# W_v and W_o folded into one product per head, summed into x by VectorE, with the later steps four half slots earlier

## What is computed

```python
# cross attention, on the normalised x, per batch
q = (query @ w_q).reshape(B, Q, 16, 64).transpose(0, 2, 1, 3)   # likewise k, v
scores = jnp.einsum('bhqd,bhkd->bhqk', q, k) * scale
attn = jax.nn.softmax(scores, axis=-1)
out = jnp.einsum('bhqk,bhkd->bhqd', attn, v)
return out.transpose(0, 2, 1, 3).reshape(B, Q, 16 * 64) @ w_o

# the routed tree, for four trees q, k, v and f
for _ in range(8):
    logit = jnp.einsum('bsd,bsd->bs', x, nw[node]) + nb[node]
    node = 2 * node + 1 + (logit > 0).astype(jnp.int32)
leaf = node - 255
h = act(jnp.einsum('bsd,bsdl->bsl', x, w1[leaf]) + b1[leaf])
return jnp.einsum('bsl,bsld->bsd', h, w2[leaf]) + b2[leaf]
```

## Time and profile before

| | us |
|---|---|
| median of 3 runs | 752.05 |
| lowest and highest run | 750.29, 752.97 |
| span of the profiled execution | 754.4 |
| PE busy in it | 597.3 (79%) |
| DVE busy | 546.0 (72%) |
| ACT busy | 406.1 (54%) |
| POOL busy | 240.9 (32%) |

### The profile page before, as it was taken

One profiled execution on the slowest core, in us unless ns is written; L12 is line 12 of the kernel. 1 busy time (PEld: TensorE's weight loads), 2 busy tenths in 40 slices (PEclk: granted clock), 3 DMA queues, 4 the chain that ended last, 5 costly groups with the idle time before them and its releaser, 6 DMA issues.

```text
span 754.4 us, 10417 instructions
## 1 busy us (share of the span) xinstructions
PE 597.3 (79%) x3928; PEld 521.6 (69%) x3928; DVE 546.0 (72%) x876; ACT 406.1 (54%) x903; POOL 240.9 (32%) x184
## 2 busy tenths in 40 slices
PE   3799999999999979779999997799999858530020
PEld 3588898899988868668978886689888747310010
DVE  2466665676666798986787798967777997737955
ACT  2476566667565557466556666665648534311420
POOL 3110000211021246740141459510523346276503
PEclk9899999999999998899999998999999989755555
DMA  9410000110000053300300174000300243034403
GB/s 230 162 40 1 2 1 1 39 45 31 1 1 1 1 199 98 107 1 1 116 2 0 40 265 158 1 1 1 116 1 2 66 168 116 1 116 168 181 0 119
DMA packets 21105, 49.03 MB, mean 65 GB/s; under 512 B 1472, under 2 KB 14144, under 8 KB 16960
## 3 DMA queue, kind: packets, MB, share of 16 engines
q0 software_dynamic: 4608, 34.74, 12.7%
q1 hardware_dynamic: 15760, 13.31, 6.2%
q10 hardware_dynamic: 688, 0.33, 0.2%
HBM read 48.10 MB, written 0.26 MB: 64 GB/s over the span
## 4 chain that ended last, share of the span: by engine, by line
PE 56%; DVE 28%; ACT 6%; issue 5%; POOL 3%; DMA 2%; ACTq 0%; DVEq 0%; POOLq 0%
PE ps_s L316 20%; PE ps_av L316 16%; PE ps_ring L427 12%; DVE chunk_max L855 5%; DVE tree L735 5%; DVE hid L714 4%; PE ps_m L316 4%; DVE pt_lo L679 3%; PE ps_ring L316 3%; DVE cur L699 3%; ACT prob L609 2%; ACT pt_hi L649 2%; DVE tree L679 1%; DVE hid L679 1%; DMA ident<-ident_in_dram 1%
## 5 line engine op out<-in xcount | busy, mean ns | idle before, releaser
L679 DVE TENSOR_TENSOR pt_lo<-ps_ring,pt_hi 128x512 fp32r<-128x512 f32 x256 | 169.7, 685 | 102.0 <-ACT pt_hi L649 102.0
L649 ACT CAST pt_hi<-ps_ring 128x512 fp32r<-128x512 f32 x256 | 145.1, 591 | 142.0 <-PE ps_ring L427 141.9
L427 PE MATMUL ps_ring<-ident,prob 128*128 128x128 f32 x1024 | 150.6, 280 | 34.4 <-DVE pt_lo L679 12.8
L609 ACT ACTIVATE prob<-ps_s,neg_max 128x1024 f32<-128x1024 f32 x128 | 141.6, 1113 | 52.2 <-DVE neg_max L876 52.0
L427 PEld LDWEIGHTS ps_ring<-ident,prob 128*128 128x128 f32 x1024 | 121.6, 146 | 65.6 <-issue 49.3
L855 DVE TENSOR_REDUCE chunk_max<-ps_s 128x1 f32<-128x1024 f32 x128 | 150.5, 1214 | 7.1 <-PE ps_s L316 7.0
L316 PE MATMUL ps_av<-pt_hi,c_hi 128*128 128x256 f32 x512 | 151.8, 296 | 0.0
L316 PE MATMUL ps_av<-pt_lo,c_hi 128*128 128x256 f32 x512 | 145.2, 284 | 0.0
L316 PE MATMUL ps_av<-pt_hi,c_lo 128*128 128x256 f32 x512 | 145.1, 283 | 0.0
L316 PE MATMUL ps_s<-ct_hi,q_hi 128*128 128x512 f32 x256 | 116.3, 454 | 4.9 <-ACT prob L609 3.9
L316 PE MATMUL ps_s<-ct_lo,q_hi 128*128 128x512 f32 x256 | 104.9, 410 | 0.0
(11 more groups left out here) (216 smaller groups left out, 739.8 us busy)
## 6 DMA issues: line engine op xcount, KB each, us to landing
stage<-ctx_t_dram SPq DMA_DIRECT2D x16, 256.0 KB, 3.1
stage<-ctx_rows_dram SPq DMA_DIRECT2D x16, 256.0 KB, 3.0
wv<-w_v_dram SPq DMA_DIRECT2D x1, 512.0 KB, 11.7
wo<-w_o_dram SPq DMA_DIRECT2D x1, 512.0 KB, 12.0
dec<-decay_dram SPq DMA_DIRECT2D x1, 512.0 KB, 7.8
nw<-node_w_dram SPq DMA_DIRECT2D x1, 510.0 KB, 8.5
nb<-node_b_dram SPq DMA_DIRECT2D x1, 510.0 KB, 8.9
wsm<-w_small_dram SPq DMA_DIRECT2D x1, 448.0 KB, 11.6
```

Of the source, the lines that this page charges most:

```text
L427: last = nc.tensor.transpose(o[:, i * P:(i + 1) * P], prob[:, n % 2, k:k + P], ident[:])
L609: nc.scalar.activation(prob[:, n % 2, 1024 * e:1024 * (e + 1)], ps_s[:, 1024 * e:1024 * (e + 1)], ACT.Exp, bias=neg_max[:, n:n + 1], accum ...
L649: nc.scalar.copy(pt_hi[:, pp, row:row + KPC, P * (n % 2):P * (n % 2 + 1)], ps_ring[:, i % 2, :].rearrange("p (k q) -> p k q", k=KPC))\
L679: return nc.vector.tensor_tensor(o, a, b_, op)
```

## The change

It computes the same in another way:
- A product `wvo` of W_v and W_o is made for each head in slots 2 to 16: PE transposes four heads of W_v (`turn0` to `turn3`, slots 2, 6, 10, 14) and multiplies by W_o (`join0` to `join3`, slots 4, 8, 12, 16), both in `ps_m` and copied by ACT at the slot's end. `wv` and `wo` are loaded into the leaf buffers, `wo` with 64 partitions.
- The odd X holds `av_sb` times `wvo`, 128 columns a head, and DVE adds it straight into `x_sb` with two SCALAR_TENSOR_TENSOR (L885, L887: PSUM times `rsum` plus x), at the top of the even slot, and frees the buffer.
- `o_sb`, `ot_sb`, the transposition, the step `proj` and the addition in `x1` are gone.
- All half-slot numbers of the later steps are 4 smaller, two slots. The numbers of `split_ct` and `split_c` are not in the tables and stay.

```diff
-POOL_AT = dict(of="Pool", xn1=45, rope=48, mask_q=48, gate=52, xl=55, xf=56, cur=57, gather_up01=59,
-               gather_down01=59, up0=61, up1=63, gather_up2=64, down0=65, gather_down2=66, up2=66, down1=67, down2=69, cur_f=72, gather3=77,
+POOL_AT = dict(of="Pool", xn1=41, rope=44, mask_q=44, gate=48, xl=51, xf=52, cur=53, gather_up01=55,
+               gather_down01=55, up0=57, up1=59, gather_up2=60, down0=61, gather_down2=62, up2=62, down1=63, down2=65, cur_f=68, gather3=73,
...
+VALUE_PE = {2: "turn0", 4: "join0", 6: "turn1", 8: "join1", 10: "turn2", 12: "join2", 14: "turn3", 16: "join3"}
...
+            def value_products(k):
...
+                    for h in range(4):
+                        last = nc.tensor.transpose(ps_m[0:DH, h * D:(h + 1) * D],
+                                                   wv[:, DH * (4 * i + h):DH * (4 * i + h + 1)], ident[:])
+                    last.then_inc(S["wv_turned"], 1)
+                else:
+                    pe.wait_ge(S["wvt_ready"], i + 1)
+                    for h in range(4):
+                        last = mm(ps_m[:, h * D:(h + 1) * D], wv_t[:, h, :], wo[:, 4 * i + h, :])
...
-                    if ot_pair(s) is not None:
-                        pe.wait_ge(S["ring_taken"], BY_ACT[("X", s - 1, 0)])
-                        last = nc.tensor.transpose(o[:, 256:256 + P], o_sb[:].rearrange("p a b -> p (a b)"), ident[:])
...
-                            last = mm(o[:, DH * j:DH * (j + 1)], av_sb[:, j * P:(j + 1) * P],
-                                      wv[:, DH * h:DH * (h + 1)])
+                            last = mm(o[:, j * P:(j + 1) * P], av_sb[:, j * P:(j + 1) * P], wvo[:, h, :])
...
+                if o_pair(s - 1) is not None:
+                    pair, i = o_pair(s - 1), RING[("X", s - 1, 0)]
+                    mine = x_sb[:, pair // PPB, :]
+                    dve.wait_ge(S["ring_filled"], i + 1)
+                    dve.wait_ge(S["rsum_ready"], pair + 1)
+                    if wqk_pair(s - 1) is not None:
+                        dve.wait_ge(S["ring_taken"], BY_ACT[("X", s - 1, 0)])
...
+                    link(nc.vector.scalar_tensor_tensor(mine, ps_ring[:, i % 2, 0:P], rsum[:, 2 * pair:2 * pair + 1],
+                                                        mine, ALU.mult, ALU.add))
+                    nc.vector.scalar_tensor_tensor(mine, ps_ring[:, i % 2, P:2 * P], rsum[:, 2 * pair + 1:2 * pair + 2],
+                                                   mine, ALU.mult, ALU.add).then_inc(S["ring_free"], 1)
```

## The result

The changed kernel takes 782.9 us (median of 4 runs, 780.1 to 784.7), the kernel before 752.5 us beside it (4 runs). The ratio is 1.040, 95% interval 1.035 to 1.044. It is slower, as forecast, but by 30 us where I had 18, and 1.9 us above the end of the range.

What follows compares the result with a forecast made beforehand. PE was taken to bound clean slots and DVE those with tree work. The terms summed to +17.8 us on the 754.4 us span, 772.2, less 2.4 for the median: 770 us, 2.4% slower, range 746 to 781 us.

Steps and rivals of the forecast that it cites:

- term 1: PE's stream, batches 0 to 2: the 16 passes of `proj` go, 1.79 us each time, -5.4 us.
- term 6: `route_v`'s walk on DVE, batches 0 to 2: held under `up0` and `up1` back to back, +15 us.
- term 8: `out1` on DVE: waits for POOL's fold behind the four splits, 2 x 2.3 = +4.6 us.
- 2, transposition and wider product: PE, 32 pairs: `o_sb`'s transposition goes, the product gets 128 columns a head, -1.3 us.
- 3 and 4, value products and X: PE, first slots: new `turn` and `join` products +5.7 us; X freed later, after the additions, +1 us.
- 5, the additions: DVE, even slots: two additions per pair, hidden in clean slots, exposed with tree work, +7.5 us (0 to 12).
- 7, the splits' new place: DVE, `hid0` and `hid1` in two batches: no longer meet splits or a fold, 2 x 3.45 = -6.9 us.
- 9, the end: Batch 3: wait for `proj` and its addition give way to two additions, -2.4 us; last 112 us unchanged.
- The rival of held additions: DVE's new additions held beside POOL, or DVE bounding clean slots too: 10 us on top, 780 us; chance 0.1.
- The median: Whole kernel: the median of runs taken as 2.4 us below the profiled span, 772.2 us becoming 770.

Runs made afterwards that it cites:

- The unshifted fold: The changed kernel with the later steps' half-slot numbers of before, still without `proj`; 770.95 us, ratio 1.018.
- one, two and four additions: Changed kernel, POOL's `up0` and `up1` waiting for `route_v`'s cast, one addition per pair left out, unchanged, or both made twice: 746.96, 751.07, 779.75 us.
- the experiment with one addition: Changed kernel, POOL's `up0` and `up1` waiting for `route_v`'s cast, second head's addition of every pair left out; 746.96 us, ratio 0.987.
- the kernel with the wait: The changed kernel with POOL's products `up0` and `up1` also waiting for `route_v`'s cast; 751.07 us, ratio 0.994.
- the later execution: The changed kernel run once more, unchanged, to look at the end; profiled span 778.1 us, ratio 1.025 from two runs.
- the kernel before with the wait: The kernel before with POOL's `up0` and `up1` also waiting for `route_v`'s cast; 746.15 us, ratio 0.986.
- `up2` held back too: The kernel before, `up0` and `up1` waiting for `route_v`'s cast, and `up2` for `out0`'s addition in batches 0 and 1; 745.37 us, ratio 0.989.

## Why the prediction was off

The sign was right, and so was the main mechanism, the walk held under two products. What failed are sizes in the sum, all but a few in the same direction: `proj` gave back 2.7 us and not 5.4 (term 1), batch 2's hold grew by 3.1 and not 0.8 (term 6), and the slot with `out1` by 4.0 and not 2.3 in each of two batches (term 8). By its own steps:

**1, `proj`.** In batch 0 the slot that held it (23, 9.94 us) answers to one of 7.92: -2.0, forecast -1.8. In batches 1 and 2 the slots are 9.60 before and 9.27 and 9.30 after: only -0.3 each. There DVE walks the tree of `route_f` of the batch before in the same slot, and `q_lo` comes behind that walk. With the 16 passes gone PE is there sooner and waits. The passes in batch 1 before, and the place after:

```profile
361.50 1.95 PE L316 MATMUL ps_m<-wo,ot_sb 128*128 128x128 f32 x16
```

```profile
359.18 1.56 DVE L710 COPY_PREDICATED cur<-right,cur 128x64 f32<-128x64 int32 x6
...
361.70 0.41 DVE L690 TENSOR_TENSOR q_lo<-ps_ring,q_hi 128x256 fp32r<-128x256 f32 x1
...
362.26 0.63 PE L419 MATMUL ps_ring<-ident,prob 128*128 128x128 f32 x4 [1.55 <-DVE q_lo L690]
```

The prediction gave all three batches the price of a slot that PE decides. In two of them DVE decided. The unshifted fold has the same two slots at 9.27 and 9.28 us, so the shift isn't the reason. This is the largest single miss after `out1`, 2.7 us.

**2, transposition and wider product.** In clean slots a pair takes 7.83 + 7.92 = 15.75 us where it took 15.94. -0.19 and not -0.04. Why it gave more than the 0.10 by which the transposition moved T0 isn't shown.

**3 and 4, value products and X.** Forecast 5.7 + 1 in all. The slots behind a `join` (5, 9, 13, 17) are 1.0 to 1.3 us longer than before, 4.6 together; those behind a W_q and W_k product (6, 8, 10, 12) about 0.5 each, 2.1 together. The busy time of PE from 60 to 142 us, with gaps where there were none, shows the second:

```profile
60.00:142.00 82.00, 80.77 (x563) 71.70 (x563) 53.41 (x90) 47.24 (x90) 0.00 (x0) 1.00 0.00 1
```

Right in sum.

**5, the additions.** Hidden in clean slots and exposed where DVE is late, as forecast. The slots behind `route` grew by 1.1, 1.6 and 1.6 us (10.20, 10.18 and 10.17 for 9.09, 8.57 and 8.57), together 4.3 for 4.5. Behind `hid0` one addition costs 0.4 us (9.41 to 9.82), so a pair about 0.8 if the first costs as much, forecast 0.75. Behind `hid1`, in the slot of `out1`, it costs nothing: 16.67, 16.68 and 16.66 us with one, two and four additions. So about 5.9 in all, forecast 7.5. (The 4.1 us of the experiment with one addition also hold 1.5 of slots 6 to 12, which are in term 4.) The clean slots were closer to the edge than the share of DVE's time had told me: 8.74 us of slack in 82 are not where the additions stand.

**6, the hold.** Batch 0 +3.7 (14.78 to 18.45), forecast 4.7; batch 1 +10.3 (8.75 to 19.00), forecast 9.5. The prediction held that the change moves nothing on the side of the gather; the gather's time differs by up to 1.2 us from one to the next, and batch 1 had been free before by a late one. That the walk is held in all three batches is the additions' doing; that batch 1 had so much to lose was in part chance. Batch 2 is a mis-sized term: the slot grew from 16.13 to 19.27, +3.1, where I had 0.8 because it was "held already". These are the rows of batch 2 after, beside the earlier trace rows:

```profile
611.45 4.68 DVE L710 COPY_PREDICATED cur<-right,lid 128x128 f32<-128x128 int32 x1
616.17 5.70 DVE L710 COPY_PREDICATED cur<-right,cur 128x64 f32<-128x64 int32 x6
...
622.23 0.41 DVE L690 TENSOR_TENSOR q_lo<-ps_ring,q_hi 128x256 fp32r<-128x256 f32 x1
```

Before, the walk stood at the end of slot 62, whose X holds no queries, since there is no pair 32; PE could do all scores of slot 63 during the hold. From `route_v`'s cast to `neg_max` that left 3.65 us. Two slots earlier X holds queries, `q_lo` stands behind the walk, and PE does the scores after it: 6.85 us. That is the whole growth. 1.25 of it are the scores behind the walk (4.90 us in the kernel with the wait), the other 1.95 PE's lower clock behind its wait of 9.3 us. I looked at what the shift moves next to each other on DVE and POOL, but not at what the ring holds in the slot that a step is moved to.

**7, the splits' new place.** Forecast -3.45 a batch; the two slots gave 0.5 and 1.4 in batch 0 and 0.4 and 1.4 in batch 1, or about 2.7 a batch once the 0.8 us of additions behind `hid0` are counted apart. `hid0` and `hid1` were free, as forecast (0.17 and 0.18 us), but `out0`'s addition stands beside `up2` now as before, and one that is let go earlier is held longer, 4.07 us for 3.06 in batch 1:

```profile
459.12 0.17 DVE L690 TENSOR_TENSOR hid<-hid,leaf 128x16 f32<-128x16 f32 x1
...
468.17 0.18 DVE L690 TENSOR_TENSOR hid<-hid,leaf 128x16 f32<-128x16 f32 x1
...
472.98 4.07 DVE L690 TENSOR_TENSOR tree<-tree,leaf 128x128 f32<-128x128 f32 x1
```

**8, `out1` waits for the fold.** Forecast +2.3 a batch; the slot grew from 12.68 and 12.67 to 16.68, +4.0 in each, near the upper bound of 4.6. The reduction of batch 1 carries the wait, and what I had left out is that its addition is then held by the next leaf's weighing and fold (DVE, then POOL):

```profile
484.87 0.34 DVE L885 SCALAR_TENSOR_TENSOR x_sb<-ps_ring,rsum,x_sb 128x128 f32<-128x128 f32 x1
...
489.34 2.02 DVE L746 TENSOR_REDUCE tree<-leaf 128x128 f32<-128x1024 f32 x1 [1.17 <-POOL leaf L981]
491.40 2.33 DVE L690 TENSOR_TENSOR tree<-tree,leaf 128x128 f32<-128x128 f32 x1
```

```profile
484.88 1.90 POOL L975 TENSOR_TENSOR leaf<-leaf,hid 128x1024 f32<-128x1024 f32 x1
486.86 2.39 POOL L981 TENSOR_TENSOR leaf<-leaf 128x1024 f32<-128x1024 f32 x1
489.19 1.90 POOL L975 TENSOR_TENSOR leaf<-leaf,hid 128x1024 f32<-128x1024 f32 x1
491.18 2.40 POOL L981 TENSOR_TENSOR leaf<-leaf 128x1024 f32<-128x1024 f32 x1
```

**9, the end.** From the last `neg_max` to x1's statistics 21.57 us for 25.05, -3.5, forecast -2.4. The rest took 115.4 for 112.2, of which 2.5 are the clock of that execution. Of the four runs behind the median two took 784.7 and 784.6 us at a mean granted clock of 0.882, two 780.1 and 781.3 at 0.888, the value of the later execution with the fast product. That half of the runs had the slow end is likely by these numbers and not shown.

**The rival of held additions** is refuted: L885 above took 0.34 us beside a weighing of POOL. By the Trainium skill ("SBUF — State Buffer", "Who interferes with whom") a DVE instruction with at most one SBUF input isn't held as long as it is outside the modes that use both ports, and one with two is held against a GpSimd instruction that reads SBUF. The additions (0.34 us), the walks and the tree additions (4.07 for 0.29 us) agree. The clips of `hid` don't fit the rule without its condition: they have one SBUF input and were held all the same, 1.20 us for 0.17 free. In which mode they were no run here shows.

**The median.** I took 2.4 us off the span, as before's three runs showed. The changed kernel's profiled span equals its median, 782.9. No run shows why the offset should carry over, and those 2.4 us alone are more than the 1.9 by which the range missed.

So the error of 13 us can be put together: `proj` in batches 1 and 2 +2.7, the hold +2.1 (-1.0, +0.8 and +2.3), batch 2's last two slots +1.0, `out1` +3.4 and the smaller relief +1.6 over two batches, the end +2.2, the median's offset +2.4 and the first 20 slots +0.4, less 1.7 in the additions and 1.0 in the slots that no term names. No single step explains the miss; that most of them point the same way does.

## What to carry over

- A DVE operation with two SBUF inputs that stands beside a GpSimd product takes the product's time. Whether it does is a race between two chains; in one batch of the kernel before 0.1 us decided over 6 us. A wait of two lines on the engine with time to spare was worth 32 us in one kernel and 9 in the other.
- The hold costs more than the product's time: PE stood still meanwhile and came back at its lower clock, up to 2.0 us more per held slot.
- What an edit takes off one engine comes back only where that engine decides. The same 16 passes of `proj` were worth 2.0 us in one batch and 0.3 in the two where PE then waited for a walk on DVE.
- When steps are moved as a block, look at what stays: splits that stood between two products, so that only one of them held the walk, and the contents of the ring in the slot that a step comes to.
- Slack read from a share of busy time isn't slack at the place of the edit. Doubling the added work and halving it shows on which side of the edge it stands.

Of all versions the kernel before with the wait is the fastest: 746.15 us, ratio 0.986 (0.980 to 0.992), or 745.37 us with `up2` held back too. With the wait the fold is about 5 us slower than without the fold, 751.07 to 746.15 (spans 749.0 and 745.5): the value products (6.7 us) and the additions cost more than `proj` and the transpositions give back.

## What the runs showed of the chip

- A held walk isn't slowed but stopped, product by product: 4.14 and 4.50 us for a first step that takes 0.31 alone, under products of 4.54 us, and 1.54 us for the six steps behind it. Two products without a gap in POOL's stream hold it for both, 9 us.
- The product on POOL isn't slowed by what it holds: 9.04 us for two with a waiting DVE, 9.13 without.
- Near the end, where PE is busy for a fifth of the time, the same 16 passes ran in 1.96 to 2.03 us in some executions and in 3.60 in others, also of one and the same kernel (granted clock 0.50 and 0.52 over the 55 us behind it, near the lower level in both). What decides it there was not found.
